# Three work orders, a PSUM bank, the row layout of the last stage and half-size transfers in a two-stage kernel

## The chip, the cores and the metric

The kernel runs on one core of a Trainium2 chip. That core has TensorE (PE), VectorE (DVE), ScalarE (ACT), GpSimd (POOL) and a queue engine that issues transfers (SP). The metric is device time in microseconds (us), lower is better. All data are float32.

## The reference, cut to what matters

`x` has 4 x 1024 tokens of 256 values. The first stage is a selective scan layer, the second a mixture of 8 experts with 2 chosen per token plus a shared expert:

```python
x = x + layernorm(scan_layer(layernorm(x)))          # D_INNER 512, 16 states, 4 taps
# scan_layer: rms norm, in_proj, silu gate, depthwise conv, dt = softplus(xc @ dt_w + dt_b),
#             h = exp(dt*A)*h + dt*B*xc over time, y = sum_s h*C + D_skip*xc, out_proj
x = x + layernorm(experts(layernorm(x)))
# experts: logits = x @ gate_w; top 2, softmax; sum of combine * (silu(x@Wg)*(x@Wu)) @ Wd
#          + (silu(x @ Sg) * (x @ Su)) @ Sd           # I 704, shared 352
```

## The kernel before

The program has three parts that follow one another.

**The scan.** The 4096 tokens are 8 chunks of 512. Each chunk has 64 slots (16 states by 4 row blocks). Every engine runs the same double loop, `loop` from -2 to 8 and slot `k` from 0 to 63: the scan of chunk `loop`, the projections of the next chunk and what comes after the previous one. Tables of slot numbers (`PROJ`, `ACT_AT`, `DVE_AT`, `POOL_AT`) give where in the slots an engine issues each step, and since each engine works strictly in its own order, an engine that waits holds back all that stands behind. In loop -1 the projections of chunk 0 are made without a scan beside them. Two things meet there. The projections go on: `bT` (the B and C projections, L534 on PE, copied by ACT in L773 and then stored and broadcast as rows), then `dt0` to `dt3` (L545 on PE, then L784, L785, L788 and L791 on ACT, and the sum L1289 and product L1298 on DVE), with the decay of the first slots (L924) and the first scans (L1222) behind. And the layer norm of the other 28 row tiles of `x` is made: DVE takes their statistics (L961, L965, `dve_stats_x(e, 1)`), POOL makes the variances (L1279, L1280), ACT the roots (L732, L734, `act_root_x(e, 1)`), POOL a Newton step (L149 to L157), and DVE then norms chunk 1 (L981). `act_root_x(e, 1)` is issued by ACT at slot 38, just ahead of the copy of `bT` in the same slot.

**The last chunk and the seam.** The eighth chunk has nothing beside it and is written out by hand in two halves of two row tiles: on PE `pe_last`. After the output projection it does, for each half, the turn of the tokens (L598), the router's `logit` (L607) and its `rank` (L615, L617), which waits for the chosen experts from DVE or POOL. Then come the shared expert's products `sg0` to `sg2` and `su0` to `su2` (L567) and `sd0`, `sd1` (L579). ACT copies `sg` out of PSUM (L911), does the silu (L858) and copies `sd` (L866); DVE multiplies by `su` (L1045). The small products and the projections take turns in three PSUM banks, A0 to A2: `bank_table` gives every product a bank and a turn, `room` makes the writer wait until the turn before has been emptied. A further bank, `bY`, holds a sum over the states of the scan and is last read before `pe_last` starts.

**The experts and the end.** 71 tiles of 128 tokens, each of one expert, go through gate and up products (L1614, banks bA and bH), a DVE multiply, a turn and the down product (L1637, banks A1 and A2). `pe_tiles` begins with waits until all three banks A have been emptied for the last time; then it loads the expert's number from `tab` into a register. The results are added in DRAM by indirect transfers (L1791). Last, 8 units of 512 rows are normed and added to the residual: SP loads the sums (L1778, 512 KB each), DVE takes statistics (L1734, L1738), POOL and ACT make roots and the norm (L1751, L1757 to L1764), DVE adds (L1746) and SP stores the unit once both halves are added (L1781). `unit_rows` maps row `j*128 + p` of a unit to partition `p`, so a partition holds four pieces of 1 KB from four places.

Of the kernel before, what the change touches and what calls it, by code (L numbers as in the profile page):

```python
# [69 lines left out]
UT = 4  # L70
# [3 lines left out]

LAST = ("y2", "y1", "y3", "y0", "logit0", "rank0", "logit1", "rank1", "sg0", "sg1", "sg2", "su0", "su1", "su2", "sd0", "sd1")

# [17 lines left out]
def bank_table():  # L94

    turn = []
    for loop in range(-2, NCH + 1):
        for k in range(SLOTS):
            for names, c, now, n in ((POST, loop - 2, SLOTS + k, NCH - 1), (PROJ, loop + 1, k, NCH), (POST, loop - 1, k, NCH - 1), (LEAD, loop + 2, k, NCH)):  # L100
                turn += [(name, c) for name in names if 0 <= c < n and slot(names, name, c) == now and not by_hand(name, c)]
    turn += [(name, NCH - 1) for name in LAST]
    return {use: (i % NQ, i // NQ + 1) for i, use in enumerate(turn)}

# [55 lines left out]
def program(nc, sem, sb, top, x_rows, out_rows, norm_w, in_proj_w, conv_w, dt_w, dt_b, A_log, B_w, C_w, D_skip,  # L160
# [124 lines left out]
    bY = bank("bY")  # L285
    A = [bank(f"A{i}") for i in range(NQ)]
    full = [sem(f"full{i}") for i in range(NQ)]
    free = [sem(f"free{i}") for i in range(NQ)]

# [320 lines left out]
    def pe_last_rank(e, h):  # L610
# [7 lines left out]
        i.then_inc(fullsem(b, CL), 1)  # L618

    def pe_last(e):  # L620
        e.wait_ge(s_scan, SLOTS * NCH)
# [8 lines left out]
        pe_last_turn(e, 0)  # L630
        pe_last_logit(e, 0)
        pe_last_rank(e, 0)
        pe_last_turn(e, 1)
        pe_last_logit(e, 1)
        pe_last_rank(e, 1)
        for t in range(NSI):
            for q in range(KD):
                pe_shared(e, f"sg{t}", w_sg, t, q, CL)
        for t in range(NSI):
# [846 lines left out]
    def act_scan(e):  # L1486
        e.preload_act_table_set(LOGEXP)
        act_root_x(e, 0)
        for loop in range(-2, NCH + 1):
# [6 lines left out]
            for k in range(SLOTS):  # L1496
# [5 lines left out]
                if 0 <= loop - 2 < CL:  # L1502
                    act_post(e, SLOTS + k, loop - 2)
                if (loop, k) == (-1, 38):
                    act_root_x(e, 1)
# [96 lines left out]
    s_x1u = sem("s_x1u"); s_acc = [sem(f"s_acc{u}") for u in range(NU)]; s_out = sem("s_out")  # L1602
    s_st = sem("s_st"); s_va = sem("s_va"); s_rl = sem("s_rl"); s_rr = sem("s_rr"); s_nn = sem("s_nn"); s_nm = sem("s_nm")
    s_no3 = sem("s_no3"); s_o = sem("s_o")
# [26 lines left out]
    def pe_down(e, t, ex):  # L1631
        e.wait_ge(s_th, t + 1)
        e.wait_ge(s_pl, t + 1)
        if t >= 2:
            e.wait_ge(s_yt, t - 1)
        for q in range(NF):
            i = e.matmul(bD[t % 2][:, 0:DM], hT[:, t % 2, q, :], arena[:, bass.ds(ex * EW + (2 * KD * FI + q * DM), DM)],  # L1637
                         start=(q == 0), stop=(q == NF - 1))
        i.then_inc(s_dn, 1)
# [86 lines left out]
    def unit_rows(d, u):  # L1726
        return d[u * UT * P:(u + 1) * UT * P, :].rearrange("(j p) d -> p j d", p=P)

    def dve_stats(e, u):
        e.wait_ge(s_acc[u], 16)  # L1730
        if u:
            e.wait_ge(s_st, 2 * u)
        for q in range(UT):
            i = e.bn_stats(st3[:, q, :], acc[:, u, q, :])  # L1734
        i.then_inc(s_st, 1)
# [30 lines left out]
    def sync_tiles(e):  # L1766
# [9 lines left out]
        e.wait_ge(s_ys, 16 * NT)  # L1776
        for u in range(NU):
            e.dma_start(acc[:, u, :, :], unit_rows(sh_d, u)).then_inc(s_acc[u], 16)  # L1778
        for u in range(NU):
            e.wait_ge(s_o, UT // 2 * (u + 1))  # L1780
            e.dma_start(unit_rows(out_rows, u), x1s[:, u, :, :]).then_inc(s_out, 16)  # L1781
        e.wait_ge(s_out, 16 * NU)

# [12 lines left out]
    def pe_tiles(e):  # L1796
        for b in range(NQ):
            e.wait_ge(free[b], max(n for i, n in PLACE.values() if i == b))
        e.wait_ge(s_tab, 1)
# [110 lines left out]
```

## Time and profile before

| | |
|---|---|
| median of 3 runs | 1633.06 us (1632.55 to 1634.78) |
| the profiled execution | 1635.02 us, its span 1633.3 us |
| busy over the span | PE 90%, DVE 84%, ACT 61%, POOL 60% |
| chain that ended last | PE 50%, POOL 16%, "issue" 14%, DVE 13%, ACT 5% |
| first scan of the first chunk starts (DVE L1222) | 60.86 us |
| first expert product starts (PE L1614) | 1065.80 us |
| last expert's result is issued (POOL L1791) | 1592.99 us |
| last store is issued (SP L1781) | 1629.9 us |

### The profile page before, as it was taken

How to read it: one execution, taken by the hardware profiler on the slowest of the kernel's cores; microseconds unless marked ns; L12 is line 12 of the kernel's file. 1: busy time of each engine (PE TensorE's matmuls, PEld its weight loads, DVE VectorE, ACT ScalarE, POOL GpSimd, SP SyncE). 2: the span in 40 equal slices, each digit the busy share in tenths (PEclk: the TensorE clock that was granted, in tenths of full speed). 3: DMA queues.
4: the chain of work that ended last, by engine and by line, in shares of the span. 5: the costliest groups of instructions: out<-in, count | busy, mean ns of one | idle time of the engine just before them, and what ended most of it. 6: DMA issues, size and time to landing. Idle time of an engine off the chain costs nothing.

```text
span 1633.3 us, 25288 instructions
## 1 busy us (share of the span) xinstructions
PE 1477.1 (90%) x6486; PEld 986.4 (60%) x6486; DVE 1379.6 (84%) x2456; ACT 989.4 (61%) x2042; POOL 977.5 (60%) x1086
## 2 busy tenths in 40 slices
PE   7788799999999999999998778799999999999990
PEld 2354556656655656755655655467777777777760
DVE  4699999899999899999999998567777777777765
ACT  3567579678679679678677564244444444444444
POOL 0478779989989889889889886211221222212124
PEclk9899899999999999999999869799999999999995
DMA  7111112311211221221211755635333323233316
GB/s 209 40 52 40 48 44 55 117 58 43 85 59 40 90 61 40 85 64 48 72 53 52 237 174 180 203 48 138 42 35 39 38 36 40 35 40 36 39 20 209
DMA packets 180748, 124.36 MB, mean 76 GB/s; under 512 B 102048, under 2 KB 157184, under 8 KB 180608
## 3 DMA queue, kind: packets, MB, share of 16 engines
q1 hardware_dynamic: 162512, 100.51, 22.8%
q0 software_dynamic: 13296, 17.97, 6.5%
q10 hardware_dynamic: 4800, 4.26, 0.8%
q8 instruction: 58, 0.95, 0.2%
q14 instruction: 82, 0.67, 0.1%
HBM read 84.72 MB, written 37.42 MB: 75 GB/s over the span
## 4 chain that ended last, share of the span: by engine, by line
PE 50%; POOL 16%; issue 14%; DVE 13%; ACT 5%; DMA 1%; DVEq 0%; POOLq 0%; ACTq 0%; SPq 0%
PE A L1637 11%; POOL arena L1395 11%; PE bA L1614 10%; PE bH L1614 10%; DVE arena L1222 7%; PE bH L708 4%; PE A L526 2%; PE A L567 2%; DVE arena_t L1239 2%; PE A L545 2%; PE A L516 2%; POOL expert_in_scratch L1383 1%; DVE arena L1239 1%; PE A L661 1%; ACT bA L924 1%
## 5 line engine op out<-in xcount | busy, mean ns | idle before, releaser
L1395 POOL TENSOR_TENSOR arena<-arena 128x512 f32<-128x512 f32 x512 | 644.7, 1276 | 102.8 <-DVE arena L1222 88.1
L924 ACT ACTIVATE bA<-arena,a_neg 128x512 f32<-128x512 f32 x512 | 352.4, 691 | 188.0 <-DVE arena L1222 181.6
L708 PEld LDWEIGHTS bH<-ident,arena 128*128 128x128 f32 x2048 | 251.5, 146 | 255.2 <-issue 118.1
L708 PE MATMUL bH<-ident,arena 128*128 128x128 f32 x2048 | 326.5, 287 | 56.0 <-DVE arena L1222 39.4
L1791 POOL DMA_INDIRECT sum_scratch<-arena_t x71 | 110.7, 1559 | 432.4 <-DVE arena_t L1854 400.1
L1222 DVE TENSOR_TENSOR_SCAN arena<-bA,arena 128x512 f32<-128x512 f32 x256 | 306.9, 1214 | 24.0 <-POOL hl L1408 13.0
L1222 DVE TENSOR_TENSOR_SCAN arena<-bA,hl,arena 128x512 f32<-128x512 f32 x256 | 321.7, 1272 | 4.7 <-ACT bA L924 4.4
L1670 ACT COPY hT<-arena_t 32x160 f32<-32x160 f32 x568 | 182.5, 321 | 227.4 <-DVE arena_t L1654 221.6
L1660 DVE STREAM_TRANSPOSE hT<-arena_t 32x192 f32<-32x192 f32 x568 | 206.0, 363 | 6.6
L1637 PE MATMUL A<-arena,hT 128*128 x852 | 197.1, 381 | 2.1 <-DVE hT L1660 2.1
L1637 PEld LDWEIGHTS A<-arena,hT 128*128 128x128 f32 x852 | 162.5, 191 | 36.2 <-issue 3.0
L1614 PE MATMUL bA<-arena,arena_t 128*128 x568 | 181.4, 463 | 2.1 <-issue 2.1
L1614 PE MATMUL bH<-arena,arena_t 128*128 x568 | 179.6, 459 | 0.0
L1846 DVE TENSOR_TENSOR arena_t<-arena_t,bH 128x352 f32<-128x352 f32 x142 | 67.6, 518 | 108.6 <-PE bH L1614 108.6
L1614 PEld LDWEIGHTS bH<-arena,arena_t 128*128 128x128 f32 x568 | 108.1, 190 | 60.3 <-issue 0.2
L1239 DVE SCALAR_TENSOR_TENSOR arena_t<-bH,bc,arena_t 128x512 f32<-128x512 f32 x180 | 131.5, 730 | 10.6 <-PE bH L708 10.1
L1614 PEld LDWEIGHTS bA<-arena,arena_t 128*128 128x128 f32 x568 | 108.6, 191 | 52.0 <-issue 3.7
L1239 DVE SCALAR_TENSOR_TENSOR arena<-bH,bc,arena 128x512 f32<-128x512 f32 x180 | 131.7, 732 | 7.0 <-PE bH L708 6.1
L526 PE MATMUL A<-arena 128*128 128x512 f32 x240 | 117.9, 596 | 2.4 <-DVE arena L974 2.4
L944 ACT ACTIVATE hs<-bH,bc 128x512 f32<-128x512 f32 x128 | 87.3, 682 | 33.6 <-PE bH L708 31.6
L567 PE MATMUL A<-arena_x 128*128 128x512 f32 (+1 forms) x192 | 98.2, 629 | 0.0
L1824 ACT ACTIVATE arena_t<-bA 128x352 f32<-128x352 f32 x142 | 58.1, 461 | 54.6 <-PE bA L1614 54.6
(251 smaller groups left out, 1857.6 us busy)
## 6 DMA issues: line engine op xcount, KB each, us to landing
arena<-b_scratch SPq DMA_DIRECT2D x128, 256.0 KB, 3.2
arena_t<-expert_in_scratch SPq DMA_DIRECT2D x564, 16.0 KB, 1.8
arena<-in_L_ffn_Wg_dram SPq DMA_DIRECT2D x8, 704.0 KB, 6.5
arena<-in_L_ffn_Wu_dram SPq DMA_DIRECT2D x8, 704.0 KB, 8.0
expert_in_scratch<-zro SPq DMA_DIRECT2D x8, 660.0 KB, 6.1
arena<-in_L_ffn_Wd_dram SPq DMA_DIRECT2D x8, 640.0 KB, 8.5
arena_x<-in_L_attn_x_dram SPq DMA_DIRECT2D x9, 512.0 KB, 5.0
arena<-in_L_attn_x_dram SPq DMA_DIRECT2D x8, 512.0 KB, 5.1
```

The lines of the kernel that those rows point to most:

```text
L526: i = e.matmul(at(b, c)[:], w_tap[:, d, q, :], xin[:, d, q:q + CH], start=(q == 0), stop=(q == TAPS - 1))
L567: i = e.matmul(at(b, c)[0:n, :], w[:, q, i0:i0 + n], xfT[:, q, :], start=(q == 0), stop=(q == KD - 1))
L708: i = e.transpose(bH[g % NH][:, q * P:(q + 1) * P], hh[:, (n - 1) % 2, q, d * P:(d + 1) * P], ident[:])
L924: e.activation(bA[g % NA][:], dt[c % 2][:, d, :], ACT.Exp, scale=a_neg[:, d, n:n + 1]).then_inc(s_a, 1)
L1222: e.tensor_tensor_scan(hh[:, n % 2, d, :], bA[g % NA][:], bb[:, k % NB, :], hl[:, n, d:d + 1] if c % 2 else 0.0, ALU.mult, ALU.add).then_i ...
L1239: e.scalar_tensor_tensor(out=yy[:, d, :], in0=bH[g % NH][:], scalar=cm, in1=yy[:, d, :], op0=ALU.mult, op1=ALU.add).then_inc(s_y, 1)
L1395: e.tensor_tensor(bb[:, k % NB, :], u[c % 2][:, d, :], br[:, n % NR, :], ALU.mult).then_inc(s_bb, 1)
L1614: i = e.matmul(banks[f][:, 0:FH], xtT[:, t % 2, k, :], arena[:, bass.ds(ex * EW + (o + k * FI + f * FH), FH)], start=(k == 0), stop=(k == ...
L1637: i = e.matmul(bD[t % 2][:, 0:DM], hT[:, t % 2, q, :], arena[:, bass.ds(ex * EW + (2 * KD * FI + q * DM), DM)], start=(q == 0), stop=(q == ...
L1660: i = e.transpose(out, in_)
L1670: i = e.copy(out, in_)
L1791: e.indirect_dma_start(out=sh_d, out_offset=bass.IndirectOffsetOnAxis(ap=xm[:].bitcast(U32)[:, t % NM, TOK - DM:TOK - DM + 1], axis=0), in ...
```

## The change

1. `act_root_x(e, 1)` moves on ACT from slot 38 of loop -1 to slot 43 (`ACT_AT["dt"][0] + 3`), behind the copies of `bT` and `bc` and the whole of `dt0`.
2. The router's four small products of the last chunk leave the turns of banks A0 to A2 and take turns in bank `bY`. This bank becomes a fourth entry of the bank and semaphore lists.
3. On PE the products `sg0`, `sg1` and `sg2` of the last chunk are made in halves of 256 tokens: the first half of `sg0` between `logit0` and `rank0`, the first half of `sg1` between `logit1` and `rank1`, the rest behind `rank1`.
4. The waits for the emptied banks at the head of `pe_tiles` go. The first two down products wait for the bank they write.
5. `unit_rows` maps row `4*p + j` of a unit to partition `p`, so a partition holds one run of 4 KB. This holds for the loads of the sums, of the residual `x1` and for the stores.
6. The first load of the sums and all stores go in halves of two row tiles (2 KB runs), 16 stores in place of 8. DVE's statistics of unit 0 start when the first half is there.

```diff
-LAST = ("y2", "y1", "y3", "y0", "logit0", "rank0", "logit1", "rank1", "sg0", "sg1", "sg2", "su0", "su1", "su2", "sd0", "sd1")
+LAST = ("y2", "y1", "y3", "y0", "sg0", "sg1", "sg2", "su0", "su1", "su2", "sd0", "sd1")
+SMALL = ("logit0", "rank0", "logit1", "rank1")
...
+    return place | {(name, NCH - 1): (NQ, i + 1) for i, name in enumerate(SMALL)}
...
+    A = [bank(f"A{i}") for i in range(NQ)] + [bY]
...
+    def pe_last_gate(e, t, h):
+        (i0, n), b, r = SIT[t], f"sg{t}", slice(2 * h * P, (2 * h + 2) * P)
+        if h == 0:
+            room(e, b, CL)
+        for q in range(KD):
+            i = e.matmul(at(b, CL)[0:n, r], w_sg[:, q, i0:i0 + n], xfT[:, q, r], start=(q == 0), stop=(q == KD - 1))
+        if h:
+            i.then_inc(fullsem(b, CL), 1)
...
         pe_last_logit(e, 0)
+        pe_last_gate(e, 0, 0)
         pe_last_rank(e, 0)
         pe_last_turn(e, 1)
         pe_last_logit(e, 1)
+        pe_last_gate(e, 1, 0)
         pe_last_rank(e, 1)
-        for t in range(NSI):
-            for q in range(KD):
-                pe_shared(e, f"sg{t}", w_sg, t, q, CL)
+        pe_last_gate(e, 0, 1)
+        pe_last_gate(e, 1, 1)
+        pe_last_gate(e, 2, 0)
+        pe_last_gate(e, 2, 1)
...
-                if (loop, k) == (-1, 38):
+                if (loop, k) == (-1, ACT_AT["dt"][0] + 3):
                     act_root_x(e, 1)
...
     def pe_down(e, t, ex):
-        if t >= 2:
+        if t < 2:
+            e.wait_ge(free[t + 1], max(n for i, n in PLACE.values() if i == t + 1))
+        else:
             e.wait_ge(s_yt, t - 1)
...
-        return d[u * UT * P:(u + 1) * UT * P, :].rearrange("(j p) d -> p j d", p=P)
+        return d[u * UT * P:(u + 1) * UT * P, :].rearrange("(p j) d -> p j d", p=P)
...
     def dve_stats(e, u):
-        e.wait_ge(s_acc[u], 16)
         if u:
             e.wait_ge(s_st, 2 * u)
+        else:
+            e.wait_ge(s_acf, 16)
         for q in range(UT):
+            if u or q == 2:
+                e.wait_ge(s_acc[u], 16)
...
-        for u in range(NU):
+        e.dma_start(acc[:, 0, 0:2, :], unit_rows(sh_d, 0)[:, 0:2, :]).then_inc(s_acf, 16)
+        e.dma_start(acc[:, 0, 2:4, :], unit_rows(sh_d, 0)[:, 2:4, :]).then_inc(s_acc[0], 16)
+        for u in range(1, NU):
             e.dma_start(acc[:, u, :, :], unit_rows(sh_d, u)).then_inc(s_acc[u], 16)
...
-            e.wait_ge(s_o, UT // 2 * (u + 1))
-            e.dma_start(unit_rows(out_rows, u), x1s[:, u, :, :]).then_inc(s_out, 16)
+            for h in range(2):
+                q = slice(2 * h, 2 * h + 2)
+                e.wait_ge(s_o, UT // 2 * u + h + 1)
+                e.dma_start(unit_rows(out_rows, u)[:, q, :], x1s[:, u, q, :]).then_inc(s_out, 16)
...
     def pe_tiles(e):
-        for b in range(NQ):
-            e.wait_ge(free[b], max(n for i, n in PLACE.values() if i == b))
         e.wait_ge(s_tab, 1)
```

In the new code the lines behind the top of the file have moved down, by 3 in `pe_last` and by 16 or more behind it. ACT in loop -1, before: the roots of the 28 row tiles (`r0`) stand ahead of the copy of `bT` (COPY 32x512).

```order
L768 COPY arena<-A2 128x512 [waits full2]
L732 ACTIVATE r0<-va 128x28 [waits s_p0v]
L734 ACTIVATE r0<-r0 128x28 [waits s_ln0]
L773 COPY arena<-A0 32x512 [waits full0]
L784 ACTIVATE arena<-A1,b_dt 128x512 [waits full1]
L785 ACTIVATE arena<-A1,b_dt 128x512
L788 ACTIVATE arena<-arena 128x512 [waits free1]
L778 COPY bc0<-A2 128x128 [waits full2]
L791 ACTIVATE arena<-arena 128x512 [waits s_ex]
L784 ACTIVATE arena<-A0,b_dt 128x512 [waits full0]
```

The same place on ACT now:

```order
L784 COPY arena<-A2 128x512 [waits full2]
L789 COPY arena<-A0 32x512 [waits full0]
L800 ACTIVATE arena<-A1,b_dt 128x512 [waits full1]
L801 ACTIVATE arena<-A1,b_dt 128x512
L804 ACTIVATE arena<-arena 128x512 [waits free1]
L794 COPY bc0<-A2 128x128 [waits full2]
L807 ACTIVATE arena<-arena 128x512 [waits s_ex]
L748 ACTIVATE r0<-va 128x28 [waits s_p0v]
L750 ACTIVATE r0<-r0 128x28 [waits s_ln0]
L800 ACTIVATE arena<-A0,b_dt 128x512 [waits full0]
```

The two roots with their wait for POOL (`s_p0v`) have moved behind six instructions, among them the copy of `bT`.

PE in `pe_last`, before, from the second turn of the tokens to the load of the first expert's number (128x8 are the logits, `bc` the chosen experts):

```order
L598 MATMUL bH<-ident,arena_x 128x128 x4
L607 MATMUL A<-w_gt,arena_x 128x8 x4
L615 MATMUL A<-bc,below 128x24
L617 MATMUL A<-bc,ones 128x16
L617 MATMUL A<-bc,ones 128x8
L567 MATMUL A<-arena_x 128x512 x4
L567 MATMUL A<-arena_x 96x512 x2
L567 MATMUL A<-arena_x 128x512 x4
L567 MATMUL A<-arena_x 96x512 x2
L579 MATMUL A<-arena_x 128x256 x12
L1609 TENSOR_LOAD tab
```

The same place on PE now:

```order
L601 MATMUL bH<-ident,arena_x 128x128 x4
L610 MATMUL bY<-w_gt,arena_x 128x8 x4
L629 MATMUL A<-arena_x 128x256 x2
L618 MATMUL bY<-bc,below 128x24
L620 MATMUL bY<-bc,ones 128x16
L620 MATMUL bY<-bc,ones 128x8
L629 MATMUL A<-arena_x 128x256 x4
L629 MATMUL A<-arena_x 96x256 x4
L570 MATMUL A<-arena_x 128x512 x4
L570 MATMUL A<-arena_x 96x512 x2
L582 MATMUL A<-arena_x 128x256 x12
L1625 TENSOR_LOAD tab
```

Two half-width products have moved ahead of the rank (two more stand in the same way ahead of the first half's rank), and the big products behind it are eight of 256 columns and six of 512 where there were twelve of 512.

## Rows read from the trace of the kernel before

**Rows 1.** Window: stretch, length, busy PE, PEld, DVE, ACT, POOL, PEclk, DMA share, GB/s.

```profile
1080.00:1587.00 507.00, 505.33 (x1933) 366.75 (x1931) 386.12 (x1040) 235.76 (x696) 107.59 (x69) 1.00 0.33 45
```

**Rows 2.** Timeline of loop -1: start, length, instruction, [idle before, releaser].

```profile
36.57 7.93 DVE L961 BATCH_NORM_STATS2 hs<-arena 128x6 f32<-128x256 f32 x24
...
41.35 3.70 PE L545 MATMUL A<-arena 128*128 128x512 f32 x8
...
48.49 0.23 ACT L732 ACTIVATE r<-va 128x28 f32<-128x28 f32 x1 [10.92 <-POOL va L1280]
...
49.49 2.08 PE L545 MATMUL A<-arena 128*128 128x512 f32 x2 [4.44 <-ACT arena L773]
...
50.80 0.24 POOL L157 TENSOR_TENSOR nmr<-mv,r 128x28 f32<-128x28 f32 x1
...
52.99 0.69 DVE L1289 TENSOR_TENSOR arena<-arena 128x512 f32<-128x512 f32 x1 [5.19 <-ACT arena L791]
...
54.32 2.33 DVE L981 TENSOR_SCALAR arena<-arena,r,nmr 128x256 f32<-128x256 f32 x4
...
63.78 0.69 ACT L784 ACTIVATE arena<-A,b_dt 128x512 f32<-128x512 f32 x1 [0.27 <-PE A L545]
...
66.39 0.69 DVE L1289 TENSOR_TENSOR arena<-arena 128x512 f32<-128x512 f32 x1 [0.88 <-ACT arena L791]
```

**Rows 3.** Windows of loop -1, columns as in rows 1.

```profile
37.50:45.00 7.50, 7.17 (x16) 2.23 (x16) 7.50 (x24) 0.07 (x1) 0.00 (x0) 1.00 0.00 0
...
49.50:56.00 6.50, 6.50 (x11) 2.83 (x12) 2.98 (x5) 2.51 (x5) 2.58 (x7) 0.50 0.51 168
```

**Rows 4.** The chain that ended last, in loop -1 and after the seam: start, length, what.

```profile
52.12 11.63 PE A L545 x22
...
1072.49 2.37 PE bA L1614 x8
```

**Rows 5.** Timeline of the last chunk's end and the seam.

```profile
1043.11 0.62 PE L615 MATMUL A<-bc,below 128*128 128x24 f32 x2 [1.88 <-DVE bc L1124]
...
1044.41 12.99 PE L567 MATMUL A<-arena_x 128*128 128x512 f32 x24
...
1057.51 0.68 DVE L1045 TENSOR_TENSOR arena_x<-arena_x,A 96x512 f32<-96x512 f32 x1 [0.53 <-PE A L567]
...
1058.29 5.43 PE L579 MATMUL A<-arena_x 128*128 128x256 f32 x24 [0.89 <-DVE arena_x L1045]
...
1063.04 0.45 DVE L1710 STREAM_TRANSPOSE arena_t<-arena_t 128x256 f32<-128x256 f32 x1 [4.14 <-DMA arena_t<-expert_in_scratch]
...
1065.80 4.32 PE L1614 MATMUL bA<-arena,arena_t 128*128 x8 [2.08 <-issue]
```

**Rows 6.** Windows at the seam, columns as in rows 1.

```profile
1036.00:1044.00 8.00, 5.13 (x23) 4.66 (x23) 2.31 (x17) 1.05 (x4) 4.18 (x10) 0.50 0.83 266
1044.50:1049.00 4.50, 4.50 (x7) 1.92 (x7) 3.96 (x20) 0.59 (x1) 2.37 (x3) 0.50 0.69 252
1050.00:1057.00 7.00, 7.00 (x18) 2.77 (x16) 2.06 (x5) 3.93 (x4) 1.15 (x2) 1.00 0.26 58
```

**Rows 7.** Timeline of the last stage.

```profile
1600.69 1.41 DVE L1734 BATCH_NORM_STATS2 st<-arena 128x6 f32<-128x256 f32 x4 [8.46 <-DMA arena<-sum_scratch]
...
1605.45 0.21 ACT L1757 ACTIVATE rr<-va 128x4 f32<-128x4 f32 x1 [1.87 <-POOL va L1752]
...
1608.67 0.20 ACT L1757 ACTIVATE rr<-va 128x4 f32<-128x4 f32 x1 [0.81 <-POOL va L1752]
```

**Rows 8.** The eight stores L1781: time from issue to landing.

```profile
DMA to landing us min/median/max: 2.9/3.0/3.8
```

**Rows 9.** Rate in 1 us slices of 0 to 40, then a window as in rows 1.

```profile
GB/s 0 12 112 363 419 393 284 68 34 57 295 369 322 375 346 365 360 295 304 349 350 347 346 348 346 352 346 350 346 270 19 0 0 0 8 0 0 0 0 0
...
1601.00:1605.00 4.00, 0.00 (x0) 0.00 (x0) 3.73 (x18) 0.41 (x2) 1.45 (x8) 0.50 1.10 348
```

**Rows 10.** Queue of SP in 1590 to 1634: packets, MB, share of 16 engines.

```profile
q1 hardware_dynamic: 8448, 8.39, 56.8%
```

More of the change, by code:

```diff
@@ L102, in bank_table @@
     turn += [(name, NCH - 1) for name in LAST]
-    return {use: (i % NQ, i // NQ + 1) for i, use in enumerate(turn)}
+    place = {use: (i % NQ, i // NQ + 1) for i, use in enumerate(turn)}
+    return place | {(name, NCH - 1): (NQ, i + 1) for i, name in enumerate(SMALL)}
 PLACE = bank_table()
@@ L285, in program @@
     bY = bank("bY")
-    A = [bank(f"A{i}") for i in range(NQ)]
-    full = [sem(f"full{i}") for i in range(NQ)]
-    free = [sem(f"free{i}") for i in range(NQ)]
+    A = [bank(f"A{i}") for i in range(NQ)] + [bY]
+    full = [sem(f"full{i}") for i in range(NQ + 1)]
+    free = [sem(f"free{i}") for i in range(NQ + 1)]
     s_w = sem("s_w"); s_w2 = sem("s_w2"); s_c = sem("s_c"); s_id = sem("s_id"); s_cst = sem("s_cst"); s_an = sem("s_an")
@@ L1602, in program @@
     s_x1u = sem("s_x1u"); s_acc = [sem(f"s_acc{u}") for u in range(NU)]; s_out = sem("s_out")
-    s_st = sem("s_st"); s_va = sem("s_va"); s_rl = sem("s_rl"); s_rr = sem("s_rr"); s_nn = sem("s_nn"); s_nm = sem("s_nm")
+    s_st = sem("s_st"); s_va = sem("s_va"); s_rl = sem("s_rl"); s_rr = sem("s_rr"); s_nn = sem("s_nn"); s_nm = sem("s_nm"); s_acf = sem("s_acf")
     s_no3 = sem("s_no3"); s_o = sem("s_o")
@@ L1776, in sync_tiles @@
         e.wait_ge(s_ys, 16 * NT)
-        for u in range(NU):
+        e.dma_start(acc[:, 0, 0:2, :], unit_rows(sh_d, 0)[:, 0:2, :]).then_inc(s_acf, 16)
+        e.dma_start(acc[:, 0, 2:4, :], unit_rows(sh_d, 0)[:, 2:4, :]).then_inc(s_acc[0], 16)
+        for u in range(1, NU):
             e.dma_start(acc[:, u, :, :], unit_rows(sh_d, u)).then_inc(s_acc[u], 16)
         for u in range(NU):
-            e.wait_ge(s_o, UT // 2 * (u + 1))
-            e.dma_start(unit_rows(out_rows, u), x1s[:, u, :, :]).then_inc(s_out, 16)
-        e.wait_ge(s_out, 16 * NU)
+            for h in range(2):
+                q = slice(2 * h, 2 * h + 2)
+                e.wait_ge(s_o, UT // 2 * u + h + 1)
+                e.dma_start(unit_rows(out_rows, u)[:, q, :], x1s[:, u, q, :]).then_inc(s_out, 16)
+        e.wait_ge(s_out, 16 * 2 * NU)
     def pool_tiles(e):
```

## The prediction

> **What bounds the kernel now.** I read the page's chain first, then the chain in order of time, then the timeline at the places that the diff touches. The scan takes the first thousand microseconds and no line of it is changed, so whatever it is bound by stays; it only starts sooner or later. The experts' part is bound by PE: 505.33 of 507 us busy at full clock [rows 1], 71 tiles of three products each, a gate product taking 2.37 [rows 4]. It too only starts sooner or later. So the change is worth what three seams lose. The chain with its stalls shows these:
>
> At the start, ACT stands still until 48.49 us, idle for 10.92 us, because the roots of the 28 row tiles wait for DVE's statistics, which run from 36.57 for 28 tiles [rows 2]. The copy of bT, whose product is ready at 41.35 where the next one starts on PE, is queued behind them. PE then stops at 45.05 (41.35 + 3.70) and waits until 49.49 with "ACT arena L773", that copy, as releaser [rows 2]. On resuming its clock is 1.2 GHz (PEclk 0.50) where it was 2.4 GHz before the halt [rows 3].
>
> At the seam, PE does the twelve shared products in 12.99 us, waits 0.89 us for DVE's last multiply, does sd in 5.43 us, then is idle 2.08 us and does its first expert product in 4.32 us [rows 5] where the later ones take 2.37 [rows 4].
>
> At the end, the units follow each other every 3.22 us (1605.45 to 1608.67, ACT waiting for POOL each time) [rows 7], and the span ends about 3.0 us after the last store is issued [rows 8].
>
> **The change part by part.**
>
> *Roots behind dt0.* I rebuild the first chunk from the lengths in the trace. PE ends dt0 at 45.05 as before. Now bT is copied at about 41.5, so PE goes on without a halt at full clock: one product of dt1, 2 records at 0.43 (3.70/8 of the row is an upper value), to 45.9; the small transposes, to 46.4; then the 22 records that follow, which took 11.63 us partly at half clock [rows 4], now 22 x 0.427 = 9.4, to 55.8. They ended at 63.75. ACT has dt0's four passes done at about 48.0, takes the roots at 48.49 as before, since they wait for DVE and POOL and not for ACT, and is free for dt1 at 49.1. The last of the four dt then starts on ACT at 55.9 in place of 63.78 [rows 2]: 7.9 us. On DVE the norm of chunk 1 (2.33 us) waits for POOL's last Newton step (50.80 + 0.24) [rows 2], so it takes 51.1 to 53.4 and holds the sum of dt1 for about 1.7 us; DVE makes this up until the last sum, which stood at 66.39 after an idle time of 0.88 [rows 2] and now follows at about 58.6: 7.8 us. What is late next is again PE's last dt, as before. I take **7.8 us**. Bounds: 5.0 if DVE does not make up its delay (dt0's sum, at 52.99 in the rows, can now start at 48.0), 8.0 from PE alone. The cost of the moved roots is nothing as long as dt1 on PE ends after 48.97, and it ends at 49.0; uncovered, they cost 0.5 us on ACT. The scan behind sees the same intervals, shifted.
>
> *Half-width gate products.* A product of 256 tokens has half the columns of one of 512, so a pair of records costs 0.43 us at full clock and 0.85 at half (1044.50 to 1049.00 holds 0.50, 1050.00 to 1057.00 holds 1.00 [rows 6]). A gate half is two of these, 1.7 us at half clock. Ahead of rank1 PE was idle 1.88 us for the chosen experts [rows 5], so the half just fits, with 0.1 to 0.2 us left; the idle time ahead of rank0 is longer. Should it not fit, rank1 is up to 0.2 us later, which holds the routing and the fetch of the first tile, not PE, as shown below. Behind rank1, two of the twelve full products' worth are gone: 2 x 0.854 = **1.7 us** at full clock, with the clock rising at the same time as before. ACT's copies and silu come sooner by more than that, so DVE's last multiply still waits for PE (1057.51 before). The lower bound is 1.2 (the halves carry their weight loads: sd's records take 5.43/24 = 0.226 us against 0.213), the upper 4.3, if the fuller PE gets its clock back before rank1 has ended: the remaining work of 8.54 us at full clock, from about 1044.5, then ends at 1053.1 and not 1055.7.
>
> *Small products in bY.* The same instructions in another bank. Their turns have logit0, rank0, logit1 and rank1 wait for the reader of the one before; each of these readers ended before PE came there. Nothing.
>
> *No waits ahead of the experts.* PE was idle from 1063.72 to 1065.80. That is the copy of sd1 by ACT (0.6) and then the load of the expert's number and the way to the first product (1.45, "issue"). Without the waits these loads can be made while the twelve sd products run; between later tiles they are made while the few matmuls of a down product run, and no idle time shows there. So **2.1 us** go. The input of the second tile stands at 1063.5 (1063.04 + 0.45 [rows 5]) and is now wanted at 1064.3 to 1066.7, two products of 2.37 behind the first; the first tile's is some 5 us older. That is a slack of 0.8 us or more. The new waits in the first two down products are met long before. If the loads were not covered, 1.45 of the 2.1 stays.
>
> *The clock behind it.* The first expert product took 4.32 us [rows 5] against 2.37 [rows 4] because the clock was at 0.50 after the idle time. PE will have only the idle 0.9 us ahead of sd, after which sd ran at full clock. I count **1.95 us**, with zero as the lower end.
>
> The Trainium skill, "TensorE: Matmul & The Clock Gate", the passage on engine queue depths, gives TensorE a queue of 64 instructions. The 24 records of sd fit into it, so by the page the expert's loads are covered; no row here shows the depth. It leaves the sum as it stands.
>
> *The end.* The first load moves 512 KB; at 348 GB/s [rows 9] that is 1.5 us, so its first half is there 0.7 us sooner, and of the four statistics (1.41 us [rows 7]) only two are left when the second half lands: 0.7 us. POOL and ACT shift by it, since the units' rhythm is their own. The last store: issued at the same distance from the last addition, with 256 KB in place of 512, so 0.75 us sooner; its first half has been issued 0.9 us before and is drained in 0.75. Together **1.45 us**. 4 KB runs were loaded at 363 to 419 GB/s (slices 4 to 6 of the row, mostly the first projection's weights) against 348 for 1 KB runs [rows 9]; that is worth 0.2 us per transfer on the path, which I leave to the range. Bounds: 0.7 (one of the halves brings nothing) and 2.3. The loads of x1 lie beside the experts and cost nothing.
>
> The rule that speaks against halves is in the Trainium skill, "DMA: Bandwidth & Descriptors", section "Rules for kernel authors": many small transfers should be joined to one large one. By its section on the anatomy of a DMA, each has a fixed cost of some 2 us. The trace shows 3.0 us from issue to landing for 512 KB, of which 1.5 are not data [rows 8, 9]; were they paid once more in line, the last store would cost 0.75 us more and not less, and the end would bring nothing. The transfers of this stage overlap, since eight are under way at once, so I don't follow it.
>
> **Sum.** 7.8 + 1.7 + 2.1 + 1.95 + 1.45 = 15.0 us. The profiled execution of 1635.02 would become 1620.0; the median of 1633.06 becomes **1618.0 us**.
>
> **The rivals.**
> - *The clock comes back earlier at the seam*, since PE's idle times between 1033 and 1044 are partly filled: 2.6 us more, 1615.4. For it: less idle time; against it: the clock stayed at 0.50 through 8 us of which PE was busy for 5.13 [rows 6].
> - *The gap ahead of the experts stays.* If the loads of the expert's number are not run ahead, 1.45 us stay and with them perhaps the slow first product: 3.4 us less, 1621.4. Against it: the gapless later tiles.
> - *The start gives only 5 us*, because DVE's norm of chunk 1 now waits for POOL in the middle of the chain: 1620.8. Against it: the idle times ahead of DVE's later sums.
> - *The moved roots do not free the chain*, that is, the stall only changes its name (DVE's statistics still being under way when dt0 is ready): 1625.8. Against it: neither the copy of bT nor dt0 on ACT needs DVE.
> - *Slower: the runs of 4 KB.* The last stage moves 8.39 MB [rows 10] in about 34 us. Should stores or loads of long runs crowd on few of the DMA engines, its length would be set by them: at 170 GB/s the 8.39 MB take 49 us and eat the 15 us, at 150 GB/s they take 56 and the kernel ends at 1640. No row shows a store of 4 KB runs; the load of such runs was fast.
>
> **How the numbers follow.** Forecast 0.57 (its own range 1616.5 to 1619.7); earlier clock 0.13; gap stays 0.14; short start 0.09; roots do not help 0.02; slower 0.03; something else 0.02, half of it near no change. The range goes from 1614.0, the early clock with the better bounds of the end, to 1622.0, the staying gap with some loss. A difference of 0.2% is about what a measurement of this kernel can tell from no change; the forecast is 0.9%.
>
> **What the new profile would show.** ACT copies bT at about 41.5; PE is not idle between 38 and 56 and at PEclk 1.00; the first scan starts near 55, the last sum of the first chunk near 58.6. Counted from rank1, sd starts 1.7 us sooner, no idle time stands ahead of the first expert product, and it takes about 2.4 us. From the last result's issue to the first statistics 7.0 us in place of 7.7, and the last store lands in 2.3 us. A first scan near 61, or a gap of over 1 us ahead of the experts, or a rate under 250 GB/s in the loads of the sums would prove me wrong.

## The result, and the profile after

| | before | changed |
|---|---|---|
| median | 1633.32 us (1632.55 to 1634.78) | 1621.7 us (1620.57 to 1623.67) |
| profiled execution | 1635.02, span 1633.3 | 1620.91, span 1619.1 |

The ratio is 0.9929 with an interval of 0.9915 to 0.9944. A later comparison of the same two kernels on one chip gave 0.9925 (0.9911 to 0.9938), medians 1622.54 and 1634.42. So the change is worth 11.6 and 11.9 us by the medians, where I had forecast 15. The direction and the places were right, the time lies at the upper end of my range (1614 to 1622) and outside the forecast's own part of it (1616.5 to 1619.7). By the time alone the rival with the gap ahead of the experts (1621.4) would fit best; the traces below rule it out.

The timeline of loop -1 in the changed kernel (start, length, instruction, [idle before, releaser]):

```profile
35.90 7.93 DVE L977 BATCH_NORM_STATS2 hs<-arena 128x6 f32<-128x256 f32 x24
...
40.68 4.56 PE L548 MATMUL A<-arena 128*128 128x512 f32 x10
40.78 0.57 ACT L789 COPY arena<-A 32x512 f32<-32x512 f32 x1 [3.88 <-PE A L537]
...
47.22 0.68 POOL L1295 TENSOR_SCALAR mv<-mv 128x28 f32<-128x28 f32 x1 [37.82 <-DVE mv L981]
...
47.96 0.59 POOL L1296 TENSOR_SCALAR va<-mv 128x28 f32<-128x28 f32 x1
48.59 0.23 ACT L748 ACTIVATE r<-va 128x28 f32<-128x28 f32 x1 [1.56 <-POOL va L1296]
48.63 1.04 POOL L1337 TENSOR_TENSOR arena<-arena,dskip 128x512 f32<-128x512 f32 x1
...
51.17 2.32 DVE L997 TENSOR_SCALAR arena<-arena,r,nmr 128x256 f32<-128x256 f32 x4 [2.69 <-POOL nmr L160]
...
53.41 0.68 DVE L1305 TENSOR_TENSOR arena<-arena 128x512 f32<-128x512 f32 x1
...
58.49 0.84 DVE L1305 TENSOR_TENSOR arena<-arena 128x512 f32<-128x512 f32 x1
...
59.37 0.69 ACT L940 ACTIVATE bA<-arena,a_neg 128x512 f32<-128x512 f32 x1 [0.91 <-DVE arena L1305]
```

Two more rows of the kernel before are needed further down, POOL's two variance operations:

```profile
47.88 0.29 POOL L1279 TENSOR_SCALAR mv<-mv 128x28 f32<-128x28 f32 x1 [38.37 <-DVE mv L965]
48.24 0.22 POOL L1280 TENSOR_SCALAR va<-mv 128x28 f32<-128x28 f32 x1
```

In the changed kernel ACT copies bT as soon as it is there, the roots wait 1.56 us and not 10.92 [rows 2], and PE does not stop. This window of the changed kernel answers to rows 3 (columns as there, PEclk third from the end): busy 18 us of 18 at full clock.

```profile
38.00:56.00 18.00, 18.00 (x51) 7.73 (x49) 15.20 (x60) 10.33 (x20) 5.79 (x10) 1.00 0.18 61
```

The seam in the changed kernel's timeline, which answers to rows 5:

```profile
1032.91 2.05 PE L629 MATMUL A<-arena_x 128*128 128x256 f32 x4
...
1034.94 0.62 PE L618 MATMUL bY<-bc,below 128*128 128x24 f32 x2
...
1036.25 6.18 PE L629 MATMUL A<-arena_x 128*128 128x256 f32 x16
...
1042.27 5.31 PE L570 MATMUL A<-arena_x 128*128 128x512 f32 x12
...
1047.69 0.68 DVE L1061 TENSOR_TENSOR arena_x<-arena_x,A 96x512 f32<-96x512 f32 x1 [0.45 <-PE A L570]
...
1048.52 5.43 PE L582 MATMUL A<-arena_x 128*128 128x256 f32 x24 [0.94 <-DVE arena_x L1061]
...
1053.79 2.53 PE L1630 MATMUL bA<-arena,arena_t 128*128 x8
```

The idle time ahead of the first expert product is gone and the product takes 2.53 us in place of 4.32. The load of the expert's number into a register (number of loads, length in ns, start) stood in the idle time before and stands inside sd now. First the kernel before, then the changed one:

```profile
L1609 PEldq TENSOR_LOAD <-tab x1: 491/491/491, 1064.6 to 1064.6; - x1
L1625 PEldq TENSOR_LOAD <-tab x1: 492/492/492, 1049.9 to 1049.9; - x1
```

The last stage, which answers to rows 7, is another matter:

```profile
1585.79 0.75 DVE L1755 BATCH_NORM_STATS2 st<-arena 128x6 f32<-128x256 f32 x2 [7.13 <-DMA arena<-sum_scratch]
...
1586.97 0.75 DVE L1755 BATCH_NORM_STATS2 st<-arena 128x6 f32<-128x256 f32 x2 [0.43 <-DMA arena<-sum_scratch]
...
1589.87 1.40 DVE L1755 BATCH_NORM_STATS2 st<-arena 128x6 f32<-128x256 f32 x4 [1.73 <-DMA arena<-sum_scratch]
...
1592.28 0.20 ACT L1778 ACTIVATE rr<-va 128x4 f32<-128x4 f32 x1 [3.07 <-POOL va L1773]
```

The second unit's statistics wait 1.73 us for their load. In the kernel before they came right behind the first unit's (started at 1600.69), and no unit waited:

```profile
1602.13 0.38 DVE L1738 BATCH_NORM_AGGREGATE mv<-st 128x2 f32<-128x6 f32 x4
1602.62 1.41 DVE L1734 BATCH_NORM_STATS2 st<-arena 128x6 f32<-128x256 f32 x4
```

The view of the stores, which answers to rows 8, shows 1.0 us less to land:

```profile
DMA to landing us min/median/max: 2.0/2.0/3.3
```

To compare traces step by step I take distances between marks, so that what went before does not matter. All in us, from the traces of the kernels named (root to map are the experiments below):

| distance | before | changed | again | root | seam | wait | tail |
|---|---|---|---|---|---|---|---|
| start of the program to DVE's 28 statistics | 36.57 | 35.90 | 36.80 | 35.86 | 36.19 | 35.58 | 36.23 |
| statistics to ACT's copy of xnT | 31.18 | 24.10 | 24.10 | 24.10 | 30.92 | 30.70 | 31.05 |
| copy of xnT to PE's first turn in `pe_last` | 961.94 | 961.58 | 962.43 | 961.52 | 961.68 | 961.48 | 961.91 |
| rank1 to sd | 15.18 | 13.58 | 13.60 | 15.15 | 13.54 | 15.16 | 15.12 |
| sd to the first expert product | 7.51 | 5.27 | 5.26 | 7.52 | 5.26 | 5.27 | 7.51 |
| first expert product to the last result's issue | 527.19 | 525.60 | 525.61 | 527.23 | 525.61 | 525.47 | 527.21 |
| last result's issue to the end | 40.31 | 39.71 | 39.63 | 40.29 | 40.13 | 40.41 | 40.43 |

The first row belongs to no part of the change: over all fourteen traces it lies between 35.58 and 37.16. The first loads do not set it (DVE's first statistics start at 4.8 to 5.3 us in all of them, PE's first projection at 13.4 to 13.9). It follows the moment at which TensorE's clock comes up in that projection. Its records are 1.1 to 1.2 us long at first and 0.6 later on, the lengths of records of this size at a PEclk of 0.50 and of 1.00. In **wait**, the earliest, three of the sixteen are long, in the traces with statistics between 35.8 and 36.8 four to six, in **pace**, the latest, seven. First **wait**, then **pace**:

```profile
13.69 8.53 PE L506 MATMUL A<-arena 128*128 128x512 f32 x16 [0.77 <-ACT arena L749]
```

```profile
13.62 10.18 PE L509 MATMUL A<-arena 128*128 128x512 f32 x16 [0.77 <-ACT arena L765]
```

The third row grows with the first (961.34 in the trace with the statistics at 35.64, 962.93 in that with 37.16); why is open. In the traces with the new order PE's first turn in `pe_last` so stands at 1021.1 to 1024.2, which is as wide as the single times of the changed kernel lie apart, and part of why the two first profiles differ by 14.1 us and the medians by 12.

### The profile page after: what moved, and what is told of

The parts are those of the page before. It is cut to its first block, busy times and chain, and to the rows that moved or that the text cites. A ratio compares the mean times of both kernels' runs of the same rounds, so it can differ in the third digit from the quotient of the medians.

```text
span 1619.1 us, 25318 instructions
## 1 busy us (share of the span) xinstructions
PE 1472.7 (91%) x6498; PEld 985.7 (61%) x6498; DVE 1379.7 (85%) x2456; ACT 989.0 (61%) x2042; POOL 978.1 (60%) x1086
## 4 chain that ended last, share of the span: by engine, by line
PE 49%; POOL 16%; issue 14%; DVE 14%; ACT 6%; DMA 1%; DVEq 0%; POOLq 0%; SPq 0%; ACTq 0%
PE A L1655 11%; POOL arena L1411 10%; PE bH L1630 10%; PE bA L1630 10%; DVE arena L1238 8%; PE bH L724 4%; PE A L529 2%; DVE arena_t L1255 2%; PE A L570 2%; ACT bA L940 1%; DVE arena L1255 1%; POOL expert_in_scratch L1399 1%; PE A L519 1%; PE A L677 1%; PE bY L739 1%
## 5 line engine op out<-in xcount | busy, mean ns | idle before, releaser
L570 PE MATMUL A<-arena_x 128*128 128x512 f32 (+1 forms) x180 | 92.7, 630 | 0.0
```

What stands on the lines that cost most here:

```text
L570: i = e.matmul(at(b, c)[0:n, :], w[:, q, i0:i0 + n], xfT[:, q, :], start=(q == 0), stop=(q == KD - 1))
```

## The experiments

**again**: the changed kernel, unaltered.

> The changed kernel once more, beside its parts on the same chip. My theory from the two traces: 8 us from the start, 5.6 from the seam, 0.6 from the end, 14 in all, and the 11.6 us of the medians come from the profiled execution of before having been a slow one of its kind (1635.0 where the median is 1633.3) and that of after a quick one (1620.9 against 1621.7): 0.9915 to 0.9935 of before. Rival: the change varies more from one execution to the next than the kernel before does, since one of its gains (the clock of TensorE at the seam) is not always had: then this profile shows a first expert product near 4 us in some executions, and single times spread over 3 us.

Measured: 1622.54 (1620.79 to 1623.46), 0.9925 (0.9911 to 0.9938) of before. Its first expert product took 2.53 us as well, and the distances that belong to the change repeat within 0.1 us. So the clock at the seam was had in both traces; the rival falls. The 14 us of my theory did not come, the medians gave 11.9. Single times still lay 2.7 us apart.

**root**: part 1 alone.

```diff
-                if (loop, k) == (-1, 38):
+                if (loop, k) == (-1, ACT_AT["dt"][0] + 3):
```

> The kernel before with part 1 alone (the roots of the 28 row tiles behind dt0). My theory: 7.4 to 8.1 us, all of them there by the first scans (last sum of the first chunk near 59 us) and kept to the end of the scan: 0.995. Rival (DVE's norm of chunk 1 in the middle of the chain): 5 us or less, 0.997; rival (the stall changes its name): 1.000.

Measured: 1626.97 (1626.75 to 1628.15), 0.9957 (0.9943 to 0.9970): 7.5 us by the medians, 7.1 by the distance up to the copy of xnT beside the first trace of before, and no less at the end of the scan. The rivals of 5 us and of none fall.

**seam**: parts 2, 3 and 4 alone; the start and the end are those of the kernel before.

```diff
+SMALL = ("logit0", "rank0", "logit1", "rank1")
...
+        pe_last_gate(e, 0, 0)
         pe_last_rank(e, 0)
...
     def pe_tiles(e):
-        for b in range(NQ):
-            e.wait_ge(free[b], max(n for i, n in PLACE.values() if i == b))
```

> The kernel before with parts 2, 3 and 4 alone (router's products in bank bY, gate products in halves, no waits ahead of the experts). My theory: 5.6 us, as the traces show them (1.6 ahead of sd, 2.2 of idle time, 1.8 of clock): 0.9966. Rival: 3.8 us, 0.9977, where the clock of the first expert product is still at 1.2 GHz.

Measured: 1628.24 (1628.06 to 1630.02), 0.9964 (0.9950 to 0.9977), 6.2 us. In the trace 1.6 + 2.25 + 1.6 = 5.5 us. The first product took 2.53, so the rival of 3.8 us falls. Parts 2 and 3 have no run of their own; their 1.6 us are the distance from rank1 to sd.

**tail**: parts 5 and 6 alone.

```diff
-        return d[u * UT * P:(u + 1) * UT * P, :].rearrange("(j p) d -> p j d", p=P)
+        return d[u * UT * P:(u + 1) * UT * P, :].rearrange("(p j) d -> p j d", p=P)
...
+        e.dma_start(acc[:, 0, 0:2, :], unit_rows(sh_d, 0)[:, 0:2, :]).then_inc(s_acf, 16)
+        e.dma_start(acc[:, 0, 2:4, :], unit_rows(sh_d, 0)[:, 2:4, :]).then_inc(s_acc[0], 16)
```

> The kernel before with parts 5 and 6 alone (4 KB runs, halves). My theory: 0.6 us, because the statistics of the second unit now wait for its load (1.73 us in the trace of after) and the rhythm of the units starts 0.4 us later, while the last store lands 1.0 us sooner: 0.9996. What I forecast was 1.45 us, 0.9991.

Measured: 1634.55 against 1634.42, 0.9998 (0.9989 to 1.0007): nothing. Its trace has the second unit later still (the same timeline view, statistics of unit 0 in two pieces, then unit 1):

```profile
1599.04 0.75 DVE L1737 BATCH_NORM_STATS2 st<-arena 128x6 f32<-128x256 f32 x2 [7.30 <-DMA arena<-sum_scratch]
1600.24 0.75 DVE L1737 BATCH_NORM_STATS2 st<-arena 128x6 f32<-128x256 f32 x2 [0.45 <-DMA arena<-sum_scratch]
...
1603.56 1.41 DVE L1737 BATCH_NORM_STATS2 st<-arena 128x6 f32<-128x256 f32 x4 [2.15 <-DMA arena<-sum_scratch]
```

The three parts apart, 7.5 + 6.2 - 0.1, are 13.6 us by their medians, the whole 11.9; with intervals of some 2 us on each, that is no contradiction.

**wait**: part 4 alone.

```diff
         e.wait_ge(s_pl, t + 1)
-        if t >= 2:
+        if t < 2:
+            e.wait_ge(free[t + 1], max(n for i, n in PLACE.values() if i == t + 1))
+        else:
             e.wait_ge(s_yt, t - 1)
...
     def pe_tiles(e):
-        for b in range(NQ):
-            e.wait_ge(free[b], max(n for i, n in PLACE.values() if i == b))
```

> The kernel before with part 4 alone (no waits for the banks ahead of the experts). My theory: the idle time of 2.08 us ahead of the first expert product goes, and with it the stretch at half clock behind it: 2.1 + 1.9 = 4.0 us, first product about 2.5 us, 0.9975. Rival: the clock had other reasons, only 2.1 us, first product still over 4 us, 0.9987.

Measured: 1631.02 against 1633.97, 0.9979 (0.9970 to 0.9988), 3.0 us with an interval of 2.0 to 4.9, between the two theories by time. The trace decides for the first. The first expert product follows sd at once and takes 2.53 us, where in the trace of **root**, which kept the waits, it took 4.32 behind an idle time of 2.09. First the timeline of **wait**, then that of **root**:

```profile
1056.35 5.43 PE L579 MATMUL A<-arena_x 128*128 128x256 f32 x24 [0.89 <-DVE arena_x L1045]
1061.62 2.53 PE L1614 MATMUL bA<-arena,arena_t 128*128 x8
```

```profile
1057.58 4.32 PE L1614 MATMUL bA<-arena,arena_t 128*128 x8 [2.09 <-issue]
```

By the distances, 2.24 + 1.72 = 4.0 us.

**rows1k**: the changed kernel with 1 KB runs.

```diff
-        return d[u * UT * P:(u + 1) * UT * P, :].rearrange("(p j) d -> p j d", p=P)
+        return d[u * UT * P:(u + 1) * UT * P, :].rearrange("(j p) d -> p j d", p=P)
```

> The changed kernel without part 5: row j*128+p of a unit on partition p again (1 KB runs), halves kept. Theory A (the long runs are what lets the second unit's load come late): the second unit's statistics start within 0.3 us of the end of the first unit's, its root 1.2 us sooner after the first statistics than in the changed kernel, last stores about 0.3 us longer in landing; in all 0.5 to 0.9 us faster than the changed kernel. Theory B (the halves and the quick issue of nine loads are the reason): the second unit is as late as in the changed kernel, time the same or slower.

Measured: 1621.65, 0.9925 (0.9911 to 0.9938), not to be told from the changed kernel. The second unit waits 1.95 us with 1 KB runs too, so theory A falls:

```profile
1585.49 1.48 DVE L1755 BATCH_NORM_STATS2 st<-arena 128x6 f32<-128x256 f32 x4 [7.36 <-DMA arena<-sum_scratch]
1587.01 0.38 DVE L1759 BATCH_NORM_AGGREGATE mv<-st 128x2 f32<-128x6 f32 x4
1589.34 1.41 DVE L1755 BATCH_NORM_STATS2 st<-arena 128x6 f32<-128x256 f32 x4 [1.95 <-DMA arena<-sum_scratch]
```

**pace**: the changed kernel with at most three loads under way.

```diff
         for u in range(1, NU):
+            if u >= 2:
+                e.wait_ge(s_acc[u - 2], 16)
             e.dma_start(acc[:, u, :, :], unit_rows(sh_d, u)).then_inc(s_acc[u], 16)
```

> The changed kernel, and each load of the sums from unit 2 on is issued when the load two units before has landed, so at most two or three are under way. Theory (the loads behind take the engines from unit 1's, since all are issued within 5 us): unit 1's statistics no longer wait, 1.2 us faster than the changed kernel. Rival (long runs are slow to start, whatever is behind them): unit 1 is as late as now, no difference.

Measured: 1620.94 (1620.47 to 1622.54), 0.9919 (0.9905 to 0.9932). The median is 0.8 and 1.6 us below the two medians of the changed kernel, the intervals overlap. In the trace unit 1 waits only 0.25 us, and 38.85 us pass from the last result's issue to the end where the changed kernel needs 39.6 to 39.7:

```profile
1591.19 1.41 DVE L1755 BATCH_NORM_STATS2 st<-arena 128x6 f32<-128x256 f32 x4 [0.25 <-DMA arena<-sum_scratch]
```

**map**: the kernel before with 4 KB runs alone.

```diff
-        return d[u * UT * P:(u + 1) * UT * P, :].rearrange("(j p) d -> p j d", p=P)
+        return d[u * UT * P:(u + 1) * UT * P, :].rearrange("(p j) d -> p j d", p=P)
```

> The kernel before with part 5 alone (4 KB runs, whole loads and stores). Theory A (long runs delay): the first statistics start at the same distance or later than in the kernel before (7.7 us behind the last result's issue), the second unit is late by over 1 us, last store in 2.7 us; 0.3 us slower to 0.3 faster. Theory B (halves are the reason): 0.3 us faster or more.

Measured: 1632.69 against 1633.97, 0.9994 (0.9985 to 1.0003), not to be told from no change. In the trace the long runs help: the first statistics start 7.15 us behind the last result's issue (before: 7.70), the units follow without a wait, and stores of 512 KB land in 2.7 us (before: 3.0 [rows 8]). From the last result's issue to the end 39.38 us, 0.9 less than before.

```profile
1598.67 1.41 DVE L1734 BATCH_NORM_STATS2 st<-arena 128x6 f32<-128x256 f32 x4 [7.99 <-DMA arena<-sum_scratch]
1600.11 0.38 DVE L1738 BATCH_NORM_AGGREGATE mv<-st 128x2 f32<-128x6 f32 x4
1600.59 1.41 DVE L1734 BATCH_NORM_STATS2 st<-arena 128x6 f32<-128x256 f32 x4
```

**whole**: the changed kernel with the first load whole again.

```diff
-        e.dma_start(acc[:, 0, 0:2, :], unit_rows(sh_d, 0)[:, 0:2, :]).then_inc(s_acf, 16)
-        e.dma_start(acc[:, 0, 2:4, :], unit_rows(sh_d, 0)[:, 2:4, :]).then_inc(s_acc[0], 16)
-        for u in range(1, NU):
+        for u in range(NU):
             e.dma_start(acc[:, u, :, :], unit_rows(sh_d, u)).then_inc(s_acc[u], 16)
```

> The changed kernel with the first load of the sums whole again; 4 KB runs and halved stores stay. Theory (halving the first load is what breaks the rate of the loads): no dip below 350 GB/s once the loads run, the first unit's four statistics start 7.15 us behind the last result's issue, the second unit's right behind them, and the span ends about 38.8 us behind that issue where the changed kernel needed 39.7: 0.9 us faster than it. Rival (the dip comes by chance, or from the quick issue of 4 KB loads): a dip here too, and an end at 39.5 or later.

Measured: 1621.25 (1618.77 to 1622.11), 0.9918 (0.9905 to 0.9932). In the trace 38.70 us at the end, as expected, 0.9 to 1.0 less than in the changed kernel. The first statistics start 7.09 us behind the last result's issue, the second unit's right behind them. The windows of 1 us (columns as in rows 1) show the rate at the point where unit 1 is loaded, in the changed kernel (last result issued at 1579.39) and in **whole** (at 1580.80):

```profile
1585.00:1586.00 1.00, 0.00 (x0) 0.00 (x0) 0.21 (x1) 0.00 (x0) 0.00 (x0) 0.50 0.94 291
1586.00:1587.00 1.00, 0.00 (x0) 0.00 (x0) 0.57 (x3) 0.00 (x0) 0.00 (x0) 0.50 0.95 133
1587.00:1588.00 1.00, 0.00 (x0) 0.00 (x0) 0.96 (x6) 0.00 (x0) 0.00 (x0) 0.50 0.87 254
```

```profile
1587.00:1588.00 1.00, 0.00 (x0) 0.00 (x0) 0.11 (x1) 0.00 (x0) 0.00 (x0) 0.50 0.95 381
1588.00:1589.00 1.00, 0.00 (x0) 0.00 (x0) 1.00 (x4) 0.00 (x0) 0.00 (x0) 0.50 0.98 295
1589.00:1590.00 1.00, 0.00 (x0) 0.00 (x0) 0.93 (x6) 0.00 (x0) 0.20 (x1) 0.50 0.89 320
```

In the changed kernel 133 GB/s at a DMA share of 0.95: the engines are taken and move little. In **whole** there is a dip too, which I had not expected, but a shallower and later one, and unit 1 does not wait.

**half3**: the changed kernel with unit 3's load in halves and unit 0's whole.

```diff
+            if u == 3:
+                e.dma_start(acc[:, 3, 0:2, :], unit_rows(sh_d, 3)[:, 0:2, :]).then_inc(s_acf, 16)
+                e.dma_start(acc[:, 3, 2:4, :], unit_rows(sh_d, 3)[:, 2:4, :]).then_inc(s_acc[3], 16)
```

> The changed kernel with unit 3's load in halves and unit 0's whole. Theory 1 (any halved load breaks the rate where it stands): loads at full rate for the first units and a dip below 300 GB/s some 3 to 4 us later than in the changed kernel. Theory 2 (only a short load at the head does it, when the engines start): no dip. In both the first two units' statistics follow each other without a wait, and the end is at 38.8 us behind the last result's issue.

Measured: 1620.88 (1618.99 to 1621.12), 0.9917 (0.9902 to 0.9932), 38.56 us at the end. Units 0 and 1 in time, and the rate falls to 250 GB/s at 8 to 9 us behind the last result's issue, in windows of half a microsecond to 213. That is 1 to 2 us later than in the changed kernel and not 3 to 4, and deeper and longer than in **whole**; the third unit waits 0.62 us. It lies between my two theories and settles neither.

**dvar**: the changed kernel with the variances of the 28 row tiles on DVE.

```diff
         i.then_inc(s_cx, 1)
+        if g:
+            pool_var_x(e, 1)
...
-                if (loop, k) == (-1, 30):
-                    pool_var_x(e, 1)
```

> The changed kernel with the two small operations of the variances of the 28 row tiles on DVE, right behind its statistics, and no longer on POOL. Theory (at the start the chain now runs through DVE's statistics, POOL's variances, slowed to 0.68 and 0.59 us beside DVE's products, POOL's skip product of 1.04 us, POOL's Newton step and DVE's norm, and holds the sums by about 0.7 us): ACT's roots come 0.5 to 1.0 us sooner, the norm of chunk 1 over 1 us sooner, the last sum of the first chunk 0.6 us sooner, no more, because ACT's passes of dt3 are next. 0.6 us faster. Rival (PE and ACT alone set it): the same time.

Measured: 1622.97 (1619.78 to 1622.99), 0.9925 (0.9912 to 0.9939), no gain in the medians. In the trace the start does what was expected. From DVE's statistics (at 36.64 here) to the copy of xnT 23.36 us in place of 24.10, and the last sum now waits for ACT:

```profile
47.90 0.18 DVE L1297 TENSOR_SCALAR mv<-mv 128x28 f32<-128x28 f32 x1
47.99 0.17 DVE L1298 TENSOR_SCALAR va<-mv 128x28 f32<-128x28 f32 x1
...
50.63 2.31 DVE L999 TENSOR_SCALAR arena<-arena,r,nmr 128x256 f32<-128x256 f32 x4 [1.09 <-POOL nmr L160]
...
58.65 0.69 DVE L1307 TENSOR_TENSOR arena<-arena 128x512 f32<-128x512 f32 x1 [0.61 <-ACT arena L807]
```

The lead is not kept through the scan. Beside the trace of **whole**, whose statistics start at 36.55, the copy of xnT is 0.64 us sooner (60.00 against 60.64). PE's next projection product starts 0.64 us sooner and ends only 0.24 sooner, as both run with PEclk at 0.50 up to some 66.5 and more of the sooner one lies in that stretch. First **whole**, then **dvar**:

```profile
61.84 5.95 PE L509 MATMUL A<-arena 128*128 128x512 f32 x8 [5.08 <-ACT arena L765]
```

```profile
61.20 6.35 PE L509 MATMUL A<-arena 128*128 128x512 f32 x8 [4.34 <-ACT arena L765]
```

The 21st scan instruction is 0.06 us sooner, and PE's first turn in `pe_last` is 0.19 us later (1023.21 against 1023.02). Besides, the end was 40.23 us long with the halved first load, unit 1 waiting 2.20 us.

**both**: dvar and whole together.

> The changed kernel with both: variances on DVE and the first load whole. Expected from theories above: 0.6 + 0.9 = 1.5 us faster than the changed kernel, some 1621.0 beside 1622.5, 0.9916 of the kernel before. Rival: 0.9925, like the changed kernel.

Measured: 1619.52 (1619.11 to 1621.28), 0.9914 (0.9901 to 0.9928), the lowest median of all: 23.35 us from the statistics to the copy, 38.60 at the end. By the medians it gains 2 to 3 us on the changed kernel, but the intervals of the ratios overlap. By the distances only the 1.0 us at the end is shown: from the statistics (at 36.18) to the last result's issue it takes 1544.02 us, between the 1543.49 of the changed kernel (statistics at 35.90) and the 1544.35 of **half3** (at 36.49), which both have the variances on POOL. The 0.75 us at the start are gone by then, as in **dvar**.

## Why the prediction was right, and where it was off

**The start** (forecast 7.8 us, measured 7.1 against the first trace of before, 6.6 to 7.1 against all five with the old order, whose distance to the copy of xnT was 30.70 to 31.18, and 7.5 by the medians of **root**). In traces whose statistics start at nearly the same moment it is less: from the statistics to PE's first turn in `pe_last` **root** (35.86) takes 985.62 us and **map** (35.80) 992.38, a difference of 6.8. The stall and its end were right: ACT no longer waits with bT queued behind the roots, PE runs on at full clock. The term was mis-sized by 0.7 us or a little more in the step on DVE's delay. I had the norm of chunk 1 hold the sums and then be made up, with PE's last dt as the next bound. It is not made up: the last sum (58.49) follows DVE's own work without idle time, and ACT waits 0.91 us for it. What I left out is that POOL's two small variance operations, 0.29 and 0.22 us before, take 0.68 and 0.59 when DVE's sum and product run beside them, which they now do; each ends 0.15 or 0.07 us behind the DVE operation beside it, and the lengths are the same in all seven traces with the new order and POOL's variances. **dvar** takes POOL out of this place and gets 0.74 us back up to the copy of xnT; then the last sum waits for ACT, as I had forecast for the change itself. It is no gain for the kernel, since the scan takes it back.

**The gate halves** (1.7, measured 1.6). The half ahead of rank1 took 2.05 us and not 1.7; it filled the idle time ahead of rank1 to the last, and the distance from the first turn to rank1 did not grow (13.42 before, 13.36 changed). The clock came back 6.2 us behind the start of rank1 before and 6.4 us now (mean PEclk 0.83 in 1049 to 1050 and 0.85 in 1041 to 1042, with 0.50 ahead of and 1.00 behind each), so the rival with the early clock (1615.4) falls. The fuller PE did not bring it back sooner.

**The waits ahead of the experts** (2.1, measured 2.24) and **the clock behind** (1.95, measured 1.6). **wait** shows both with nothing else changed. The first two products got 1.8 us back; 0.2 of it was lost again in the very last down product, which took 4.54 us in place of 4.30 after its idle time (in **wait** it took 2.85). The trace shows the load of the expert's number while sd runs, at 1049.9, 1.4 us behind sd's start. The Trainium skill, "TensorE: Matmul & The Clock Gate", the passage on engine queue depths, gives TensorE a queue of 64 instructions. The trace agrees with that as far as the load does not wait for sd's 24 records; it does not show the depth. The rival that kept the gap falls.

**The end** (1.45, measured 0.6 and 0.7 in the two traces, nothing in **tail**). The store half was right, even low: 1.0 us for 0.75, of which the halving alone gives 0.8 (2.2 us to land in **rows1k**, with 1 KB runs) and the long runs 0.2. The load half was wrong. The step that failed is "POOL and ACT shift by it, since the units' rhythm is their own": the first unit's root came 0.77 us sooner behind the last result's issue in the first trace, and the second unit's 0.43 us later than before, because its load was late, and the rhythm counts from there. In six traces with the halved first load, unit 1 waited 0.2 to 2.2 us; in the eight others no unit 1 waited. A rate under 250 GB/s in the loads of the sums was one of the signs that I had named against me, and it came (133). The rule of the Trainium skill to join many small transfers ("DMA: Bandwidth & Descriptors", section "Rules for kernel authors"), which I had set aside, was right in its result for the first load and wrong for the stores. The fixed cost that I had named beside it stands in that page's section on the anatomy of a DMA for transfers issued by GpSimd, and these are issued by SP. A fixed cost paid again is not what the trace shows. The cost came with a loss of rate, 133 GB/s with the engines taken in the changed kernel, where **whole** had 381 at nearly the same distance from the last result.

The slower rival falls: in the trace of **map** the 4 KB runs do better than 1 KB runs in the first load, the rate and the landing of the stores, and its time is not above the kernel's before.

By the traces the terms are 7.1 + 1.6 + 2.24 + 1.6 + 0.65 = 13.2 us (12.7 to 12.9 with the shorter starts of the other traces), so some 1.8 of the 15.0 were not there, 0.7 at the start, 0.8 at the end and 0.3 in the clock. The medians give 12. The remaining 0.8 to 1.6 us lie within their intervals (10 to 14.5 us by the second comparison), and no step of the traces shows them.

**Open.** Why a halved first load lowers the rate. It is neither the length of the runs (**rows1k** has it) nor only the quick issue of the loads (**map** issues its eight in 3.7 us without it). **pace** softens it. A weaker dip also appears with a whole first load, and moving the halves to unit 3 moved the dip by less than the distance of the loads. I did not try other ways to cut the load, by partitions for instance. Nor is it shown why the scan is longer in the traces with late statistics, or that the small products in bank bY cost nothing by themselves.

## What to carry to other kernels

A step that waits for something slow belongs in an in-order engine's program behind the work that is ready, and when it is moved, look for what then runs beside its other steps: here two small POOL operations went from 0.51 us together to 1.27 and were the new chain. A lead at the start counts only where it is still there at the end of the stage: that of **dvar** was down to 0.06 us at the 21st scan instruction. Where TensorE was about to enter a long dense part, a wait of 2.2 us at its door cost 4.0, once as idle time and once as half clock behind it. Halving the last store, whose landing is the end of the program, gave 0.8 us, but look at what the transfers behind a halved first load do before counting the gain.

## What was not expected of the hardware

POOL operations of 128x28 elements took 0.29 and 0.22 us beside an idle DVE and 0.68 and 0.59 us beside DVE's sum and product of 128x512, and ended just behind them. Eight loads of 512 KB were issued by SP in 3.71 us with 4 KB runs (**map**) and in about 7 us with 1 KB runs, and moved at 395 GB/s (**map**, 1598 to 1604) against 348 [rows 9]. A store of 256 KB in 2 KB runs landed in 2.0 us, in 1 KB runs in 2.2 (**rows1k**), one of 512 KB in 4 KB runs in 2.7, one of 512 KB in 1 KB runs in 3.0. The moment at which DVE's 28 statistics start varied from 35.6 to 37.2 us between executions of programs that are alike up to there, with the moment at which TensorE's clock came up: after three long records of the first projection in the earliest and seven in the latest.
